# Moving two layer-norm sums and two scan groups behind the first matmuls of the last LoRA and down units

## The reference

```
h = layernorm(x) * (1 + ca) + sa
x = x + ga * mamba(h)            # a scan over the tokens: 16 states for each of 1024 channels
h = layernorm(x) * (1 + cb) + sb
gate = h @ gate_w.T + lora(h, gate_a, gate_b)      # 1024 -> 2752
up   = h @ up_w.T   + lora(h, up_a, up_b)
hidden = silu(gate) * up
x = x + gb * (hidden @ down_w.T + lora(hidden, down_a, down_b))   # 2752 -> 1024
```

## Time and profile before

| | before |
|---|---|
| median of 3 runs | 2279.3 us (2279.28 to 2288.31) |
| profiled execution: time, span | 2278.67 us, 2276.9 us |
| PE busy, instructions | 2028.3 us (89%), 11502 |
| POOL, DVE, ACT busy | 68%, 63%, 46% |
| granted PE clock, mean | 0.947 |

### The profile page before, as it was taken

How to read it: one execution, slowest core, us unless ns; L and a number is a source line. 1 busy time by engine, 2 the same in 40 slices (tenths; PEclk the granted TensorE clock), 3 DMA queues, 4 the chain that set the end, 5 groups by cost and what they waited for, 6 DMA issues and landing times.

```text
span 2276.9 us, 32700 instructions
## 1 busy us (share of the span) xinstructions
PE 2028.3 (89%) x11502; PEld 1835.2 (81%) x11502; DVE 1445.3 (63%) x2119; ACT 1043.3 (46%) x2334; POOL 1540.9 (68%) x959
## 2 busy tenths in 40 slices
PE   7587757887778889989999999999999999999999
PEld 4233226777768889889899898899889999999999
DVE  4675776778666688766778765778757774211111
ACT  3776855656553455454555444555444332210000
POOL 1488879998987877977877866877869886110100
PEclk9788877989989999999999999999999999999999
DMA  9799876777867577666667576667577877787786
GB/s 361 283 376 339 318 273 215 276 266 276 285 231 286 192 266 264 245 242 251 208 237 264 203 255 238 208 237 263 205 246 262 275 247 269 249 300 265 257 289 217
DMA packets 120051, 594.13 MB, mean 261 GB/s; under 512 B 10448, under 2 KB 22992, under 8 KB 80208
## 3 DMA queue, kind: packets, MB, share of 16 engines
q1 hardware_dynamic: 119888, 592.04, 73.8%
HBM read 506.97 MB, written 85.03 MB: 260 GB/s over the span
## 4 chain that ended last, share of the span: by engine, by line
PE 54%; DVE 18%; ACT 9%; issue 7%; POOL 6%; DMA 5%; DVEq 0%; ACTq 0%; SPq 0%; POOLq 0%
PE FP L789 46%; DVE ring L1211 7%; DVE ring L1096 3%; PE FP L672 3%; POOL ring L1332 3%; ACT SC L868 2%; DMA raw<-w_gu 2%; DVE FP L1186 2%; PE FP L750 1%; POOL y L1307 1%; DMA wts<-w_scratch 1%; PE FP L814 1%; ACT sqb L986 1%; DVE hb L1171 1%; ACT wts L889 1%
## 5 line engine op out<-in xcount | busy, mean ns | idle before, releaser
L789 PE MATMUL FP<-xhi,wts 128*128 128x368 f32 (+2 forms) x4224 | 1052.0, 325 | 76.4 <-ACT dtb L991 23.0
L789 PEld LDWEIGHTS FP<-xhi,wts 128*128 128x128 f32 x4224 | 754.3, 193 | 86.4 <-issue 71.3
L1332 POOL TENSOR_TENSOR ring<-ring,c_row 128x736 f32<-128x736 f32 (+2 forms) x336 | 575.3, 1712 | 256.3 <-ACT hst L885 256.2
L789 PE MATMUL FP<-xlo,wts 128*128 128x368 f32 (+2 forms) x2112 | 683.4, 324 | 0.0
L868 ACT ACTIVATE SC<-dtb,aneg 128x368 f32<-128x368 f32 (+2 forms) x768 | 409.4, 538 | 577.4 <-DVE ring L1211 576.9
L789 PE MATMUL FP<-hhi,wts 128*128 128x368 f32 (+5 forms) x2376 | 573.9, 322 | 15.6 <-POOL hlo L1348 5.1
L1211 DVE TENSOR_TENSOR_SCAN ring<-SC,hst,ring 128x368 f32<-128x368 f32 (+1 forms) x640 | 580.0, 948 | 4.2 <-ACT SC L868 3.8
L1307 POOL TENSOR_TENSOR y<-y,ring 128x736 f32<-128x736 f32 (+1 forms) x320 | 555.1, 1735 | 13.9
L789 PEld LDWEIGHTS FP<-hhi,wts 128*128 128x128 f32 (+1 forms) x2376 | 409.3, 186 | 23.8 <-issue 8.5
L789 PEld LDWEIGHTS FP<-xlo,wts 128*128 128x128 f32 x2112 | 408.0, 193 | 1.1
L789 PE MATMUL FP<-hlo,wts 128*128 128x368 f32 (+5 forms) x1188 | 380.1, 320 | 0.0
(11 more groups left out here) (109 smaller groups left out, 1915.9 us busy)
## 6 DMA issues: line engine op xcount, KB each, us to landing
wts<-w_scratch SPq DMA_DIRECT2D x243, 1152.0 KB, 5.2
wts<-w_scratch SPq DMA_DIRECT2D x91, 896.0 KB, 4.9
wts<-w_scratch SPq DMA_DIRECT2D x51, 1024.0 KB, 5.6
w_scratch<-wts SPq DMA_DIRECT2D x43, 1152.0 KB, 8.5
raw<-w_gu SPq DMA_DIRECT2D x43, 576.0 KB, 6.7
modw<-mod_w SPq DMA_DIRECT2D x24, 1024.0 KB, 11.2
w_scratch<-wts SPq DMA_DIRECT2D x16, 896.0 KB, 6.2
w_scratch<-wts SPq DMA_DIRECT2D x9, 1024.0 KB, 8.1
```

The source lines that it names most:

```text
L789: last = mm(out, w, x, start=(start and k == 0 and e == 0), stop=(stop and k == n - 1 and e == 2))
L1332: G.tensor_tensor(buf, buf, over_pair(c_of(k)), ALU.mult).then_inc(g_hc, 1)
```

## The change

In chunks 0 to 3 the lists at the end of a pass were one list in front of unit 62: `cen` 2 and 3, `grp` 5, `sq`, `sq2`, `grp` 6, `grp` 7. Now unit 62 keeps `cen` and `grp` 5; unit 63 has `sq`, `sq2`, `grp` 6; unit 64 has `grp` 7. In chunk 4, `sq` and `sq2` stay with unit 62 and `rstd` goes from unit 62 to unit 64. Chunk 5 has no pieces. PE does the "begin" of units 63 and 64 (`LATE_PIECES`) ahead of their pieces and the "end" of the unit before behind them; DVE does the pieces of these units ahead of `used`; POOL's and ACT's loops take the shorter lists, and ACT does the pieces of unit 63 ahead of its part of unit 62. `bank_plan` walks the new order.

```diff
+LATE_PIECES = [LAST_LORA + 1, LAST_LORA + 2]
...
 def pieces_at(c):
...
-    for u in (LAST_LORA + 1, LAST_LORA + 2):
-        at[LAST_LORA] += at[u]
-        at[u] = []
...
-            order += PIECES[c][u] + [("unit", c, u)]
+            order += [("unit", c, u)] + PIECES[c][u] if u in LATE_PIECES else PIECES[c][u] + [("unit", c, u)]
...
-            g = item[1] * NU + item[2] + (2 if UNITS[item[2]][0] == "gate" or item[2] == LAST_LORA else 1)
+            g = item[1] * NU + item[2] + (2 if UNITS[item[2]][0] == "gate" or item[2] in (LAST_LORA, LAST_LORA + 1) else 1)
... (PE)
+                    if u in LATE_PIECES:
+                        unit(c, u, "begin")
                     for p in PIECES[c][u]:
                         piece(p)
-                    if u == LAST_LORA:
-                        for v, step in ((u, "begin"), (u + 1, "begin"), (u, "end"), (u + 2, "begin"), (u + 1, "end"), (u + 2, "end")):
-                            unit(c, v, step)
-                    elif u not in (LAST_LORA + 1, LAST_LORA + 2):
+                    if u in (LAST_LORA, *LATE_PIECES):
+                        unit(c, u if u == LAST_LORA else u - 1, "begin" if u == LAST_LORA else "end")
+                        if u == LATE_PIECES[-1]:
+                            unit(c, u, "end")
+                    else:
                         unit(c, u)
... (ACT)
+                    for p in PIECES[c][u]:
+                        piece(p)
                     if u and last == "lora_down":
                         after(c, u - 1)
-                    for p in PIECES[c][u]:
-                        piece(p)
... (DVE)
-                    if g and last != "gate":
+                    if g and last != "gate" and u not in LATE_PIECES:
                         used(*divmod(g - 1, NU))
-                    if UNITS[u][:2] == ("down", len(PARTS) - 1) and UNITS[u][2] == 0:
-                        lora_low(c)
                     for p in PIECES[c][u]:
                         piece(p)
+                    if u in LATE_PIECES:
+                        used(*divmod(g - 1, NU))
+                    if u == LATE_PIECES[0]:
+                        lora_low(c)
```

## The result

| | before | after |
|---|---|---|
| median | 2277.6 us (20 runs, 2270.77 to 2288.31) | 2270.19 us (20 runs, 2260.45 to 2282.38) |
| ratio, 95% interval | | 0.9967, 0.9952 to 0.9982 |
| profiled execution: time, span | 2278.67, 2276.9 us | 2263.51, 2261.7 us |

7.4 us are gained, between 4 and 11 by the interval. Single executions of one kernel spread over 18 to 22 us, so the 15 us between the two profiled ones are not the change's size: 1.6 us of them are there before unit 61 of pass 0 ends, ahead of all that was moved. From the end of unit 61 to the start of the next pass, passes 0 to 3 take 48.5, 47.8, 47.1 and 47.3 us, where they took 50.9, 47.1, 50.4 and 50.5: 2.4, -0.7, 3.2 and 3.2 us, in sum some 8 of the 15.

A forecast was written before the change was run, and what follows sets the result against it. PE, busy 2028.3 of 2276.9 us, was the bound, leaving idle time and low clock to win. Passes 0 to 3 gain 2.8, 0.2, 1.5, 1.4 us, plus 0.1 each in 2 and 3: 6.1 us, giving 2273.2; range 2266.5 to 2281.

The forecast's parts named there:

- Step 1 and 2: Before 62 begin: squares' wait (2.75 to 5.12 us) goes, a wait for block 20's `hlo` replaces it; 5.8 us won.
- Step 3: Before 62 end and unit 65: waits for block 21's `hlo` (0.37 to 2.09 us) and the bank (0.29) go.
- Step 4: PE in the tails: one stall instead of three saves restarts, 0.3 us each, 1.2 in all.
- Step 5: PE's clock behind the new stalls: half speed behind all four at the old price, so no gain.
- Rival A: Clock stays up behind shorter stalls: 2269.6 us if in passes 2 and 3 alone, 2265.6 in all four; chance 0.20.
- Step 6: DVE, group 7 after `lora_low`: `rstd` 1.8 us later against PE; in pass 1 only 0.2 of 1.1 us remain.
- Step 7: Pass 0, unit 68's wait for weights follows 62 end: 2.5 us gain and 0.3 for restarts, 2.8 us.
- Rival B: Passes 1 to 3, `lora_low` to `used` of unit 68: group 7 on DVE sets the end; 2283.4 us; chance 0.10.
- C: Later waits (weights, `xlo`, late groups in the next pass) take back what is won: 2279 us within 1.5; chance 0.12.

The follow-up runs named there:

- Groups alone: Groups 6 and 7 moved as in the changed kernel, both sums of squares left in front of unit 62; 2271.84 us, ratio 0.9958 to the kernel before.
- sums alone: PE in the changed order, ACT, DVE and POOL in the order of before; 2301.1 us, ratio 1.0093 to the kernel before.
- the second profile: The changed kernel run again with nothing altered, for a second profile; 2264.13 us.
- Block 20 early: Changed kernel with ACT's high and POOL's low half of block 20 ahead of unit 61's pieces; 2254.92 us, ratio 0.989; second run 2257.37 us, 0.9915.

## Why the prediction was right

The forecast was 2273.2 us with no difference above 0.5%; measured were 2270.2 and a ratio of 0.9967. The 6.1 us of gain lie inside the interval of 4 to 11. (1.7 of the 3.0 us between the two times are the kernel before, whose median is 2277.6 over 20 runs where I had 2279.3 over three.) Up to the next pass's start I forecast 2.8, 0.2, 1.5 and 1.4 us for passes 0 to 3; the profile has 2.4, -0.7, 3.2 and 3.2. So the waits were right and the clock was not, and that the sum came near is in part luck: the clock cost about 1 us more in pass 1 and 3.6 less in passes 2 and 3. By its steps:

- *Step 1 and 2, one wait for another.* The last part of the hidden width has eight blocks, 14 to 21, not seven: a unit there has 24 matmuls, a "begin" 21, and the cover of step 1 is 42 matmuls, not 36. In pass 3 they take 7.1 us, from 1631.37 to 1638.46, and the squares are there in time. The stalls were to be 4.75, 3.43, 2.81 and 2.78 us, and were 4.87, 3.53, 2.91 and 2.86. The 5.8 us won in idle time were 19.53 - 14.16 = 5.4.
- *Step 3.* Both waits are gone. The experiments add what the prediction did not say: of the two halves of the change this is the one that pays. Groups alone give a ratio of 0.9958, sums alone 1.0093; the intervals leave room for a few us that the sums may add or take. In the idle times the sums' part is 14.3 us of waits for squares against 14.2 now, that is nothing.
- *Step 4, restarts.* Pass 3 is busy for 17.25 us at full clock, against 19.34 - 1.8 = 17.5 before: 0.3, as forecast.
- *Step 5, the clock, was mis-sized.* I took half speed behind all four stalls at the old price. In passes 2 and 3 the clock stayed at 1.00, worth 1.8 us each; in pass 1 it was low for longer: PE is busy for 18.27 us there, against 15.50 with no stall, 2.8 us instead of 1.8. Rival A in its form for passes 2 and 3 is what happened, and its 2269.6 is nearer to the median than my 2273.2. I had weighed 2.86 us as near to 3.22 and set it against 2.47. The premise, that length decides, fails in the kernel before itself: the stall of 2.51 us in the earlier trace rows was followed by half speed, as its first matmul of 0.59 us shows, and I left it out. The rule that I cited from the Trainium skill (TensorE: Matmul & The Clock Gate, "Why this matters for your kernels"), that gaps above about 3 us are to be avoided, agrees with the tails in all three profiles of the changed kernel, and not with the windows above, where 2.9 us was enough. It does not agree with the kernel before either, where 2.34, 2.51 and 2.75 us were enough.
- *Step 6, DVE in pass 1.* As computed: `rstd` was to begin 7.6 us behind the start of 62 end, and DVE, not PE, to set when unit 68 is taken over. 62 end starts at 975.86 and line 1162 at 983.39, 7.5 us later. The give-back is 0.85 us of lag, which comes back as 0.94 us more wait for `xlo`. The "0.2 us remain" holds where the clock is low for one stretch, as I assumed: the second profile has 0.3. With the longer low clock pass 1 loses time: from the end of unit 61 to the end of the next pass's first unit it takes 54.66 us, against 52.69 before and 53.78 in the second profile.
- *Step 7, pass 0.* The wait for weights in front of unit 68 is 3.58 us (3.87 before): it follows 62 end. The gain at the end of unit 68 is 5.15 - 1.58 (the lead at the end of unit 61) = 3.6 us, where 2.8 were forecast; 1.2 us of it are given back by the start of pass 1, whose wait for `xlo` is 4.75 us instead of 3.99, so 2.4 remain. That wait is not group 7's doing, for it is 4.74 us with group 7 in its old place as well; its cause stays open.
- *Rival B and C.* In passes 2 and 3 the next pass's wait for `xlo` is 2.34 and 2.51 us, as before to 0.01: nothing was given back there. C describes a third of pass 0's gain at unit 68 and no more. B was right in its place, pass 1, and wrong in its reach.

## What to carry to other kernels

When work is moved out from in front of a wait, ask which operand is the next to be late, and what that one is queued behind: here 3 us of waiting for squares became 3 us of waiting for a low half that POOL and ACT could have made 5 us sooner, and two small changes of their order took twice as much off the time as the change did. Split a change that moves several things before judging it: one half of this one can't be told from all of it, the other alone costs 0.9%. A producer's queue and the order of its consumer are one design: PE's late broadcast blocked the product behind which PE itself then waited.

## What the runs showed of the hardware

A stall of TensorE of 2.9 us, at the same place with the same length to 0.01 us, was followed by about 3.4 us at 1.2 GHz in two kernels and by none in a third. Shorter ones went both ways: in before 2.34, 2.51 and 2.75 us were followed by it and 2.47 us was not; in the changed kernel 2.34 and 2.51 us, at the same places, were not. A longer one need not bring it: in the second run of "Block 20 early" PE stood still for 3.61 us in front of unit 68, and the clock stayed at 1.00 behind it:

```profile
664.49 0.38 PE L787 MATMUL FP<-hhi,wts 128*128 128x256 f32 x1 [3.61 <-DMA wts<-w_scratch]
```

```profile
664.49:667.90 3.41, 3.28 (x25) 3.02 (x25) 3.41 (x6) 3.13 (x7) 2.87 (x2) 1.00 1.00 316
667.90:671.31 3.41, 3.04 (x24) 2.90 (x24) 2.89 (x4) 2.99 (x7) 3.41 (x3) 1.00 0.84 335
```

The price where it came was 1.8 us, and 2.8 when it lasted through two such stretches (960.80 to 967.60 in the changed kernel, clock 0.50). The mean clock from 620 us to the end is 0.98 in the profiles of before, of the changed kernel and of groups only; by an estimate from this figure that is 50 to 80 us at half speed in 1650. Where they fall may be part of the 18 to 22 us by which executions of one kernel differ, which was not measured.
